# A token slot reordered on all engines: patch means one slot ahead, score halves parted, turned tokens and logits in the recurrence's bank

## The reference

```python
red = x.mean(over the 16 pixels)                       # patch mean, 256 channels
q = ln(red) @ Wq.T;  kv = ln(pixels) @ Wkv.T           # 8 heads of 32
h = red + softmax(q k) v @ proj.T + b                  # over the 16 pixels of the position
h = concat(cls_tok, h)                                 # 257 tokens an image
h = h + scan(tanh(ln(h) @ W_ih.T + b + state @ W_hh.T))  # a recurrence over the 32 IMAGES
h = h + moe(ln(h))                                     # top 2 of 8 experts, gelu; moe adds its own input
```

## Time and profile before

| | us |
|---|---|
| runs of the kernel, median of 3 | 1630.0 |
| lowest, highest | 1616.41, 1631.88 |
| span of the profiled execution (first to last instruction) | 1531.7 |
| the profiled execution's own time | not printed by the profile |
| median of the runs less that span | 98.3 |
| PE busy in the span | 1341.8 (88%) |
| DVE, ACT, POOL busy | 1036.9, 819.7, 710.8 |
| mean granted TensorE clock | 0.962 of full |
| DMA moved | 423.68 MB, 277 GB/s |

### The profile page before, as it was taken

The page is one execution under the profiler, slowest core; times in us unless marked ns, Lnnn a source line. Parts: engine busy times, 40 slices in busy tenths (PEclk is TensorE's granted clock), DMA queues, the critical chain, the costliest instruction groups (busy, mean ns, idle before and its releaser), DMA issues. The chain is left out here.

```text
span 1531.7 us, 61774 instructions
## 1 busy us (share of the span) xinstructions
PE 1341.8 (88%) x25169; PEld 1084.1 (71%) x25169; DVE 1036.9 (68%) x2724; ACT 819.7 (54%) x1999; POOL 710.8 (46%) x853
## 2 busy tenths in 40 slices
PE   3889998989999999999989989888996899989970
PEld 2577776777777777777777767766775789967860
DVE  3567665766767776787866766667776577578884
ACT  0455554555555555555555555555556577755640
POOL 1333433333333334333355556555332177777376
PEclk9899999999999999999999999999999899999995
DMA  8978777787877887787888989899633488989897
GB/s 276 380 244 303 282 270 256 274 297 249 306 282 265 295 299 288 266 288 269 300 288 284 333 301 310 309 308 323 244 130 101 162 287 288 298 271 334 289 291 225
DMA packets 186613, 423.68 MB, mean 277 GB/s; under 512 B 23968, under 2 KB 89312, under 8 KB 186208
## 3 DMA queue, kind: packets, MB, share of 16 engines
q1 hardware_dynamic: 172288, 381.58, 72.1%
q0 software_dynamic: 14048, 38.16, 7.8%
HBM read 332.26 MB, written 87.39 MB: 274 GB/s over the span
## 5 line engine op out<-in xcount | busy, mean ns | idle before, releaser
L1099 DVE BATCH_NORM_STATS2 st<-xp 128x6 f32<-128x512 f32 x512 | 340.2, 696 | 0.5
L640 POOL TENSOR_TENSOR rs_px<-px_ve,half_neg 128x16 f32<-128x16 f32 x64 | 186.1, 2908 | 305.8 <-DVE px_ve L1104 305.8
L742 ACT ACTIVATE zT<-bank 128x512 f32<-128x512 f32 x256 | 139.3, 597 | 68.6 <-PE bank L957 67.4
L735 ACT ACTIVATE z_s<-bank 128x512 f32<-128x512 f32 x256 | 138.7, 597 | 64.1 <-PE bank L947 64.1
L916 PE MATMUL bank<-xc,u 128*32 128x64 f32 x8192 | 143.6, 220 | 27.7 <-issue 27.3
L916 PEld LDWEIGHTS bank<-xc,u 128*32 128x32 f32 x8192 | 129.0, 110 | 51.5 <-issue 40.7
L716 ACT ACTIVATE u<-bank 128x512 f32<-128x512 f32 x256 | 132.1, 603 | 51.6 <-PE bank L895 51.6
L957 PE MATMUL bank<-ident,z_s 128*128 128x128 f32 x1024 | 155.9, 287 | 4.4 <-issue 3.5
L1363 POOL DMA_INDIRECT y<-ys_dram,slot x130 | 129.4, 995 | 59.3 <-issue 34.7
L412 POOL DMA_INDIRECT xs_dram<-xrow,slot x130 | 130.0, 1000 | 41.0 <-issue 36.8
L947 PE MATMUL bank<-xp,pd 64*32 64x256 f32 x4096 | 126.1, 381 | 3.2 <-ACT u L716 3.2
(11 more groups left out here) (179 smaller groups left out, 3196.4 us busy)
## 6 DMA issues: line engine op xcount, KB each, us to landing
xp<-xpix SPq DMA_DIRECT2D x256, 512.0 KB, 6.5
xc<-xg SPq DMA_DIRECT2D x256, 512.0 KB
xc<-xs_dram SPq DMA_DIRECT2D x86, 256.0 KB, 4.4
ys_dram<-y_s SPq DMA_DIRECT2D x86, 256.0 KB, 4.1
xs_dram<-zero SPq DMA_DIRECT2D x57, 384.0 KB
base_dram<-h SPq DMA_DIRECT2D x65, 128.0 KB, 8.1
rows_dram<-tok SPq DMA_DIRECT2D x65, 128.0 KB, 7.8
hb<-base_dram SPq DMA_DIRECT2D x65, 128.0 KB, 3.5
```

The lines of the kernel that those rows point to most:

```text
L640: pool.tensor_tensor(rs_px[:, :], px_ve[:, :], half_neg[:, :], ALU.pow).then_inc(s["px_done"], 1)
L735: act.activation(z_s[:, r, 2 * half:2 * half + 2, :].rearrange("p a c -> p (a c)"), BIG[2 * r + half][:, :], ACT.Copy).then_inc(s["z_done" ...
L742: act.activation(zT[:, c, :, :].rearrange("p h (a r t) -> p r h a t", r=2, t=TS)[:, r, :, :, :], BIG[f][:, :].rearrange("p (a h t) -> p h ...
L1099: dve.bn_stats(st[:, j, :], xp[u.x][:, 2 * j:2 * j + 2, :].rearrange("p i c -> p c i")).then_inc(s["st_done"], 1)
```

## The change

Every engine's slot list gets a new order, and there is one more slot, k = -1.

- The unit's means, mean_out, mean_stats, mean_scale, mean_norm and mean_base are done one slot ahead of the rest of its front: in slot k for unit k+1 (`ahead`, unit n).
- token_norm moves from the slot of `end` to the end of the slot of `back`, behind token_out.
- PE: the first score half opens the slot, the second comes behind turn_xn, the four turn_z, turn_rn and recur. turn_p follows project_out, then turn_h, turn_rs, weigh. means stands between project and project_out.
- DVE: seven statistics and the token's own stand before the unmask; the softmax steps follow one another without statistics between.
- POOL: the token's scale and base come first; mean_base and mean_scale come last but for the slot's second scatter row; its first is ahead of pixel_scale.
- ACT and SP follow: exps behind a_out, all four z_out together at the end; the row and base are stored ahead of the xp loads.
- turned tokens and logits go to RB, with waits on hT_done and lg_done that keep the uses of RB apart; means loses its waits on lg_done and rk_done (turn_rn has the latter).
- In ACT's list route_exp and ranks_out move to the slot of the next piece, at its head.

```diff
 def over_slots(eng, slot):
-    for k in range(UNITS + 3):
-        slot(eng, Unit(0, k), k < UNITS, 0 < k <= UNITS, 1 < k <= UNITS + 1, 2 < k <= UNITS + 2, k > 3)
+    for k in range(-1, UNITS + 3):
+        slot(eng, Unit(0, k), k < UNITS - 1, 0 <= k < UNITS, 0 < k <= UNITS, 1 < k <= UNITS + 1, 2 < k <= UNITS + 2, k > 3)
 def group_of(t):
...
     return [(g, k - FIRST[g] - SIZES[g] - 4) for g in GROUPS[:-1] if 0 <= k - FIRST[g] - SIZES[g] - 4 < 8]
+
+
+def ranked_before(k):
+
+    return sum(FIRST[g] + SIZES[g] + 4 + 4 < k for g in GROUPS[:-1])
 def weights_now(k):
...
         FB, SB, AB, RB, BIG = pbank[0], pbank[1], pbank[2], pbank[3], pbank[4:8]
+        turned_tok, tok_logits = RB[:, 0:C], RB[:, C:C + E]
         names = """consts_in mem_set prep_pe prep_act prep_dve cls_pe cls_dve cls_pool w_ready
...
             pool.tensor_tensor(h2[t % 2][:, :], h2[t % 2][:, :], tok[t % 2][:, :], ALU.add).then_inc(s["base_done"], 1)
-        def turn_tok(pe, t, bank):
+        def turn_tok(pe, t, turned):
             pe.wait_ge(s["tok_done"], t + 1)
             if t == UNITS - 1:
                 pe.wait_ge(s["h2_done"], T_ALL)
             if t >= UNITS - 1:
                 pe.wait_ge(s["lg_done"], t)
-            if t + 4 < UNITS:
-                pe.wait_ge(s["qT_done"], 2 * (t + 5))
             for c in range(CC):
-                last = pe.transpose(bank[:, c * P:(c + 1) * P], tok[t % 2][:, c * P:(c + 1) * P], ident[:, :])
+                last = pe.transpose(turned[:, c * P:(c + 1) * P], tok[t % 2][:, c * P:(c + 1) * P], ident[:, :])
             last.then_inc(s["et_ps"], 1)
-        def logits(pe, t, bank):
+        def logits(pe, t, lg):
             pe.wait_ge(s["tokT_done"], t + 1)
+            if t > 0:
+                pe.wait_ge(s["lg_done"], t)
             for c in range(CC):
-                last = pe.matmul(bank[:, 256:256 + E], tokT[:, c, :], rw_s[:, c, :], start=(c == 0), stop=(c == CC - 1))
+                last = pe.matmul(lg, tokT[:, c, :], rw_s[:, c, :], start=(c == 0), stop=(c == CC - 1))
             last.then_inc(s["lg_ps"], 1)
...
                         sp.dma_start(w2_in_s[:, e, :, :], w2[e].rearrange("(c p) n -> p c n", p=P)).then_inc(w2_in, 16)
+                if late:
+                    keep_row(sp, t)
+                    keep_base(sp, t)
                 if mid and v.k + XBUF < UNITS:
...
                         load_tile(sp, 0, k, k)
-                if late:
-                    keep_base(sp, t)
-                    keep_row(sp, t)
             over_slots(sp, slot)
...
                 pool.tensor_copy(clsH[:, :, bass.ds(b, 1)], hT[0][:, :, P:P + 1]).then_inc(s["clsH_done"], 1)
-            def slot(pool, u, front, mid, back, end, late):
-                w, z = u.before(2), u.before(3)
-                if front:
-                    mean_scale(pool, u)
-                    mean_base(pool, u)
+            def slot(pool, u, ahead, front, mid, back, end, late):
+                n, w, z = u.before(-1), u.before(2), u.before(3)
+                rows = scatter_now(u.k)
                 if late:
                     route_scale(pool, u.k - 4)
+                    route_base(pool, u.k - 4)
+                if end and z.two == 0:
+                    keep_cls(pool, z)
+                for t in rows[:1]:
+                    scatter(pool, t)
                 if front:
                     pixel_scale(pool, u)
                 if back:
                     token_scale(pool, w)
-                if end and z.two == 0:
-                    keep_cls(pool, z)
-                if late:
-                    route_base(pool, u.k - 4)
-                for t in scatter_now(u.k):
+                if ahead:
+                    mean_base(pool, n)
+                    mean_scale(pool, n)
+                for t in rows[1:]:
                     scatter(pool, t)
...
                     act.activation(dst[:, e, :, :], src[:, e, :, :], ACT.Copy, scale=WSC).then_inc(s["w_hi"], 1)
-            def slot(act, u, front, mid, back, end, late):
-                v, w, z = u.before(), u.before(2), u.before(3)
-                if front:
-                    mean_out(act, u)
+            def slot(act, u, ahead, front, mid, back, end, late):
+                n, v, w, z = u.before(-1), u.before(), u.before(2), u.before(3)
+                if end:
+                    xn_out(act, z)
+                for g, part in pieces_now(u.k):
+                    if part == 1:
+                        route_exp(act, g)
+                    if part == 5:
+                        ranks_out(act, g, FB)
                 if back:
-                    zT_out(act, w, 0)
-                if back:
-                    zT_out(act, w, 1)
+                    for f in range(4):
+                        zT_out(act, w, f)
                 if front:
                     rn_out(act, u)
+                if end:
+                    hidden(act, z)
+                if front:
+                    q_out(act, u)
+                if late:
+                    route_turned(act, u.k - 4, turned_tok)
                 if back:
-                    zT_out(act, w, 2)
-                    zT_out(act, w, 3)
+                    a_out(act, w)
+                if late:
+                    route_logits(act, u.k - 4, tok_logits)
                 if mid:
                     exps(act, v)
                 if front:
-                    q_out(act, u)
-                if end:
-                    xn_out(act, z)
-                if back:
-                    a_out(act, w)
-                if front:
                     u_out(act, u)
-                if late:
-                    route_turned(act, u.k - 4, FB)
-                if end:
-                    hidden(act, z)
-                if late:
-                    route_logits(act, u.k - 4, FB)
-                if mid:
-                    z_out(act, v, [0, 1])
-                for g, part in pieces_now(u.k):
-                    if part == 0:
-                        route_exp(act, g)
-                    if part == 4:
-                        ranks_out(act, g, FB)
+                if ahead:
+                    mean_out(act, n)
                 if front:
                     rep_out(act, u)
                 if mid:
-                    z_out(act, v, [2, 3])
+                    z_out(act, v, range(4))
                 for k in weights_now(u.k):
...
                 wait(pe, s["qT_done"], u, 2, 0)
-                wait(pe, s["lg_done"], u, 1, -4)
-                ranked = sum(FIRST[g] + SIZES[g] + 4 + 4 < u.k for g in GROUPS[:-1])
-                if ranked:
-                    pe.wait_ge(s["rk_done"], ranked)
                 for q in range(4):
...
                 wait(pe, s["hT_done"], z, 2, 2)
+                wait(pe, s["lg_done"], z, 1, 0)
                 for c in range(CC):
                     last = pe.transpose(RB[:, c * P:(c + 1) * P], hT[z.two][:, c, 0:P], ident[:, :])
                 last.then_inc(s["ht_ps"], 1)
-            def slot(pe, u, front, mid, back, end, late):
-                v, w, z = u.before(), u.before(2), u.before(3)
-                if front:
-                    means(pe, u)
+            def slot(pe, u, ahead, front, mid, back, end, late):
+                n, v, w, z = u.before(-1), u.before(), u.before(2), u.before(3)
                 if mid:
                     score(pe, v, 0)
-                if back:
-                    turn_z(pe, w, 0)
-                    turn_z(pe, w, 1)
-                if mid:
-                    score(pe, v, 1)
-                if back:
-                    turn_z(pe, w, 2)
-                if front:
-                    turn_rn(pe, u)
-                if back:
-                    turn_z(pe, w, 3)
-                if mid:
-                    fold_patches(pe, v)
                 if end:
                     turn_xn(pe, z)
+                if back:
+                    for f in range(4):
+                        turn_z(pe, w, f)
                 if front:
-                    queries(pe, u)
-                if back:
-                    values(pe, w)
-                if front:
-                    project(pe, u, back)
-                if mid:
-                    turn_p(pe, v)
-                if late:
-                    turn_tok(pe, u.k - 4, FB)
+                    if ranked_before(u.k):
+                        pe.wait_ge(s["rk_done"], ranked_before(u.k))
+                    turn_rn(pe, u)
                 if end:
                     recur(pe, z, 0)
                     recur(pe, z, 1)
+                if mid:
+                    score(pe, v, 1)
+                if front:
+                    queries(pe, u)
+                if mid:
+                    fold_patches(pe, v)
+                if late:
+                    wait(pe, s["hT_done"], z, 2, 2)
+                    turn_tok(pe, u.k - 4, turned_tok)
+                if back:
+                    values(pe, w)
+                if late:
+                    logits(pe, u.k - 4, tok_logits)
```

(51 more changed lines are left out.)

18 lines of the change are left out of this document (9 added, 9 removed).

## The result

The changed kernel takes 1684.8 us (median of 4 runs, 1671.89 to 1692.75) against 1626.95 us (4 runs, 1616.41 to 1631.88): ratio 1.0392, with a 95% interval of [1.0334, 1.0449]. It is slower by 3.9%, and the forecast of 1632 us with its range of 1602 to 1657 us was wrong.

The account below looks back on a forecast made before the run. PE was taken as the bound. Clean slots +8, scatter -10, routing pieces +9 and tail -5 summed to +2 us on the 1531.7 us span; with 98.3 us carried around it, 1632 us, range 1602 to 1657.

Parts of the forecast that it names:

- Clean slots, +8: Some 44 slots outside scatter and start: 16.5 us each, 0.2 above now, less 1 for holes in PE's supply; +8 us.
- the two loops: In a clean slot, PE's own cycle of 16.4 us and the loop through DVE and POOL of 16.5 us.
- Scatter slots, -10: 15 slots with scatter: q_rs no longer waits behind the indirect DMAs, 0.7 us less each; -10 us.
- DMA engines, 17.2 us: In scatter slots the DMA engines are what is late next, so a clean one takes 17.2 us.
- Routing pieces, +9: Pieces last in DVE's slot, now ahead of the chain to the unmask: first group +6, second +3; +9 us.
- Tail, -5: Last slots: token_norm ahead of the weights' splitting cuts PE's 8.49 us wait by about 4, with 1 the slot before; -5 us.
- Start, 0: Slot -1 holds only the first means, which also came first before: 0 us.
- 98.3 us around the span: Gap between the profiled span of 1531.7 us and the median, carried unchanged into the forecast time.
- PE alone pacing: Rival 1: the wait before turn_rs is half, DVE's loop closes at 16.1 us; -27, 1603 us; chance 0.25.
- The port block: Rival 2: DVE and POOL block each other, token_norm and mean_scale serialise behind mean_base; +25, 1655 us; chance 0.2.
- the sign that I had named for this rival: token_norm or mean_norm on DVE taking 0.8 us instead of 0.4 would speak for rival 2.
- the third rival: Holes in PE's supply move as weigh and score stand back to back: 1652 us, or 1622; chance 0.1 by itself.

Follow-up runs that it names:

- the repeated execution of before: The kernel before, unedited, profiled once more: 1627.66 us, with a span of 1625.6.
- e8: Changed kernel with two of the seven statistics ahead of the unmask moved behind it: 1677.25 us.
- e3: Changed kernel with turn_p ahead of project_out on PE: 1661.53 us.
- e10: Changed kernel with the slot's first scatter row behind pixel_scale instead of ahead of it: 1642.27 us.
- e2: Kernel before with the slot's first scatter row ahead of pixel_scale, the second last: 1605.87 us.
- e11: Kernel before with the token slots' 62 indirect DMAs replaced by plain ones of the same bytes, first group's tokens unsorted: 1575.32 us, one run.
- e7: Changed kernel with the routing pieces ahead of spread_p on DVE instead of last in the slot: 1667.79 us.

## Why the prediction was wrong

By its own steps, with the repeated execution of before as the base, since that is the one of typical length (56 us more between slots 0 and 63, 57.9 in the medians). Two terms of the sum carry the miss: scatter slots by 27 us and routing pieces by 22.

- **Clean slots, +8: right.** 29 plain slots grew by 0.37 us, +11, where two executions of one kernel differ by 0.16. The wait at turn_rs was put at 0.5 and is 0.66; DVE's stand before pd "about 2" and is 2.88; mean_norm's wait for POOL 0.5 and is 0.44; the clean slot 16.5 and is 16.82. I took the two loops as equally long; e8 shows that DVE's is not the one that sets the slot, e3 that PE's wait alone is worth 23 us. That 1.0 us of ready PE work stood directly ahead of turn_p was in my own list of rows.
- **Scatter slots, -10: wrong, the failing step.** The prediction saw the half of the indirect DMAs that "move to mid-slot" and asked only what they no longer delay: q_rs. It costed the first row, put ahead of pixel_scale, at nothing. What it issues takes 2.3 us of POOL, and before that POOL waits 3 to 9 us for a transfer that SP issues in the same slot. That makes rs_wide late, and PE waits 3.2 us a slot plus the clock behind it. e10 removes just this and gives 42 us. Measured against before it is +17 (15 slots of 0.9, and 3.6 in the slot of k = 43). It is not more because the clock was already low in before's scatter slots (PE is busy 18.79 us a slot there and 18.31 in the changed kernel), and the parted issues may give back some 1.5 us a slot at the same time, an estimate from e2 (21.12 to 19.59). The bound "DMA engines, 17.2 us" was wrong too, by e11.
- **Routing pieces, +9: the mechanism right, the size a third.** Measured +31: 2.42 us in each of the 8 first slots and 2.96 in each of the last 4. I took 14 us of pieces, fully exposed, less what these slots already had lost in the profile; but PE has no slack left when the fold is late, and behind some of its waits the clock halves: PE is busy 17.44 us in such a slot and 16.43 in a plain one, where before it was 16.38 and 16.19, so about 0.8 us a slot is clock. The second group, put at +3, cost 12 in its last four slots. e7 and e8 give 17 and 8 us back, from these slots. The term was right in kind; its size left out the clock.
- **Tail, -5: not seen.** The 8.49 us wait of the earlier trace rows is now 2.24 us at turn_xn and 3.16 at turn_tok, about 3 less, as foretold. The second block's first transpose comes 61.3 us after the last rT, 56.4 before, but in the new order that rT stands a good part of a slot earlier. From the last weigh, which has the same place in both, it is 27.1 against 28.2 us: 1.1 gained of the 5. What takes up the rest of the 3 us was not followed up; PE's wait for its own sequencer just ahead of that transpose is 3.08 us instead of 0.74. All that lies behind the last rT is 449.0 against 451.3 us.
- **Start, 0:** -3 us.
- **98.3 us around the span: not there.** It did no harm to the sum, which was made of differences, but it hid that the earlier trace rows show an execution whose scatter slots are 2.7 us shorter than typical ones. A span that lies 6% under the median of the runs should have told me not to trust a 10 us term from just these slots.

**The rivals.** PE alone pacing (1603 us) was wrong for the clean slot. The port block (1655 us) too, for the clean slot: L1136, with both its inputs in SBUF, takes 0.29 us in the middle of rs_px's 2.92 us (509.79 against 509.32 to 512.24), and token_norm 0.44 beside rc where 0.41 is usual. But the sign that I had named for this rival, token_norm at 0.8 us, is there in 13 of the 15 scatter slots, where POOL is late and both start together:

```profile
883.60 0.72 POOL L639 TENSOR_TENSOR rc<-rT,cvec 128x256 f32<-128x256 f32 x1
```

```profile
883.67 0.80 DVE L1180 TENSOR_SCALAR xn<-h_s,hmv,h_rs 128x256 f32<-128x256 f32 x1 [1.71 <-POOL h_rs L658]
```

It loses 0.4 us of 0.65 us of overlap. No cost of it shows: later in such a slot DVE stands idle before the unmask (2.92 us at 871.08, behind a token_norm of 0.81 us at 860.96). The Trainium skill, "SBUF — State Buffer", section "Who interferes with whom", calls the port pair that DVE and GpSimd share an exclusive lock, by which L1136 would have waited for the end of rs_px; its row doesn't agree, and the slowed token_norm does so only in part.

Holes in plain slots did not grow: 0.56 us a slot against 0.88. Holes did matter, but in before's scatter slots, where the third rival did not look, and through the clock more than by their length.

## What to carry to other kernels

When an instruction is moved ahead of another on an in-order engine, its own waits are moved too: look up what releases it, when that was issued and when it lands, and ask who needs the instruction behind it. A loss may need two moves that cost little each (a row ahead of a power, a transpose ahead of its cover), so price the slack that each takes from the other. Check first that the profiled execution's span is near the runs' median, and if it isn't, trust no small term from the stretches where they may differ.

## What was unexpected of the hardware

- PE's supply of instructions has holes of some 0.4 to 0.5 us, and one of 1.12 in the slot shown, while POOL issues indirect DMAs: 60 holes of 29.2 us over 15 slots, 0.88 us a slot in all with plain DMAs of the same bytes (e11) against 2.31. That the indirect DMAs bring them is shown by one run; by what path is not. The first execution of before had the same issues and only 5 holes at them; why, stays open.
- Such holes cost more in clock than in length: the same matmuls take 18.79 us a slot with them (granted clock 0.90 of full in 850 to 1060 us), 16.37 in the first execution (0.99) and 16.26 with plain DMAs (0.98).
- Behind each of the fourteen waits of 2.86 to 4.43 us on PE the granted clock fell to its lower level for a time: weigh 3.67 us instead of 1.96 at 883.34. Behind waits of 1.3 to 2.7 us it did so in some slots and not in others, and behind the 0.66 us of each clean slot it did not (1.96 at 499.24).
- With the DMA engines 0.92 busy and 326 GB/s, scatter slots lasted 17.36 us on average (e11), hardly longer than quiet ones (17.14).
